# Row maxima to the stacked queries: a copy for all heads and one-hot key rows, in place of two DMAs per step

## What is computed

```python
x = x + _L0_xattn_ref(_layernorm(x), ctx_1024, ctx_1024)
x = x + _L0_ffn_ref(_layernorm(x), ...)       # 64 experts, top 8
x = x + _L1_xattn_ref(_layernorm(x), ctx_1024, Wq, Wk, Wv, Wo)   # causal
x = x + _L1_ffn_ref(_layernorm(x), ...)
# both attentions:
scores = jnp.einsum('bqhd,bkhd->bhqk', q, k) * scale
out = jnp.einsum('bhqk,bkhd->bhqd', jax.nn.softmax(scores, axis=-1), v)
```

## Time and profile before

| | |
|---|---|
| profiled execution | 1326.34 us |
| its span, first to last instruction | 1324.5 us |
| mean granted TensorE clock | 0.848 |
| median of three runs | 1323.26 us |
| TensorE busy, share | 971.9 us, 73% |
| VectorE busy, share | 614.0 us, 46% |
| ScalarE busy, share | 361.3 us, 27% |
| GpSimd busy, share | 487.8 us, 37% |
| first attention, first to last scores | 78.5 to 279 us |
| second attention, first to last scores | 926.9 to 1135 us |

### The profile page before, as it was taken

How to read it: one execution, slowest core, us unless ns; L and a number is a source line. 1 busy time by engine, 2 the same in 40 slices (tenths; PEclk the granted TensorE clock), 3 DMA queues, 4 the chain that set the end, 5 groups by cost and what they waited for, 6 DMA issues and landing times. The chain is left out here.

```text
span 1324.5 us, 22383 instructions
## 1 busy us (share of the span) xinstructions
PE 971.9 (73%) x5670; PEld 644.4 (49%) x5671; DVE 614.0 (46%) x1831; ACT 361.3 (27%) x884; POOL 487.8 (37%) x500
## 2 busy tenths in 40 slices
PE   4658687661003999999999999932667688589999
PEld 3525344430002666666666666622455466346665
DVE  4548776745001444444444444415777675232230
ACT  4526444430001222122222222210244345222221
POOL 4500332455563767676767767610000000000000
PEclk9959867865555999999999999975688789779999
DMA  5954564200004555665665666424556532200000
GB/s 179 294 140 135 78 89 67 45 21 11 0 0 122 182 179 189 188 195 165 189 196 182 205 206 198 153 102 167 156 153 195 156 92 70 78 0 16 17 15 17
DMA packets 78845, 160.32 MB, mean 121 GB/s; under 512 B 18448, under 2 KB 44048, under 8 KB 76480
## 3 DMA queue, kind: packets, MB, share of 16 engines
q1 hardware_dynamic: 59264, 112.16, 30.0%
q0 software_dynamic: 19520, 47.41, 11.5%
HBM read 118.09 MB, written 41.16 MB: 120 GB/s over the span
## 5 line engine op out<-in xcount | busy, mean ns | idle before, releaser
L1204 PE MATMUL ex_ps<-ex_w_gu,ex_rows_t 128*128 x640 | 263.2, 493 | 27.5 <-issue 17.0
L834 POOL DMA_INDIRECT expert_lists<-rt_number,rt_idx x128 | 124.4, 972 | 200.2 <-DMA expert_lists<-rt_number,rt_idx 116.0
L1173 POOL DMA_INDIRECT expert_outs<-ex_result,slot_places x160 | 158.7, 992 | 100.4 <-DVE ex_result L1316 98.3
L649 ACT ACTIVATE a_probs<-a_ps 128x512 f32<-128x512 f32 (+1 forms) x256 | 133.7, 541 | 167.6 <-PE a_ps L514 84.5
L494 PE MATMUL a_ps<-stacked_keys,a_qst 96*128 96x256 bf16 (+1 forms) x512 | 119.2, 307 | 77.9 <-DMA stacked_keys<-k_stack 57.6
L1168 POOL DMA_INDIRECT ex_rows<-moe_rows,slot_tokens x160 | 155.1, 970 | 56.9 <-issue 48.8
L1223 PE MATMUL ex_ps<-ex_w_down,ex_hidden_t 96*128 x640 | 166.8, 383 | 1.0 <-DVE ex_hidden_t L1308 1.0
L1658 POOL TENSOR_TENSOR x<-x,ff_b 128x256 f32 x16 | 11.5, 747 | 387.1 <-DVE ff_xn L1814 387.1
L1278 ACT ACTIVATE ex_act_g<-ex_ps 128x192 f32<-128x192 f32 x160 | 52.8, 330 | 353.7 <-PE ex_ps L1204 353.7
L511 PE MATMUL a_ps<-a_qst,stacked_keys 98*128 98x256 bf16 (+1 forms) x512 | 114.8, 298 | 27.8 <-DMA a_qst<-a_maxrows 18.7
L1204 PEld LDWEIGHTS ex_ps<-ex_w_gu,ex_rows_t 128*128 128x128 f32 x640 | 108.5, 192 | 43.3 <-issue 36.1
(11 more groups left out here) (210 smaller groups left out, 1341.6 us busy)
## 6 DMA issues: line engine op xcount, KB each, us to landing
ex_w_gu<-in_w_gu_dram SPq DMA_DIRECT2D x64, 384.0 KB, 3.2
cb_gathered<-expert_outs SPq DMA_DIRECT2D x16, 1024.0 KB, 7.7
ex_w_down<-in_w_down_dram SPq DMA_DIRECT2D x64, 192.0 KB, 3.7
k_stack<-split_parts SPq DMA_DIRECT2D x16, 384.0 KB, 2.6
a_qst<-q_stack SPq DMA_DIRECT2D x32, 192.0 KB, 4.5
stacked_keys<-k_stack SPq DMA_DIRECT2D x32, 192.0 KB, 4.6
a_qst<-q_stack SPq DMA_DIRECT2D x32, 128.0 KB, 4.4
stacked_keys<-k_stack SPq DMA_DIRECT2D x32, 128.0 KB, 4.4
```

The source lines that it names most:

```text
L649: nc.scalar.activation(probs[:, s, 0:cols], ps[:, 2 + s % 2, 0:cols], ACT.Exp, scale=scale).then_inc(exped, 1)
L834: nc.gpsimd.indirect_dma_start(k.lists, bass.IndirectOffsetOnAxis(ap=self.idx[:, t, s:s + 1], axis=0), self.number[:, t, s:s + 1], None).t ...
L1173: nc.gpsimd.indirect_dma_start(k.outs, bass.IndirectOffsetOnAxis(ap=k.places[:, begin + t:begin + t + 1], axis=0), result[:, t % R], None) ...
L1204: last = pe.matmul(ps[:, 2 + j % 2, 0:2 * FF], rows_t[:, j % 2, c * P:(c + 1) * P], w_gu[:, bass.ds(ring, 1), c, :].rearrange("p a n -> p ...
```

## The change

`MROWS` becomes 16: all 16 rows of the transposed maxima (2 parts x 8 heads) become rows 96 to 111 of `qst`. ScalarE copies them there from PSUM directly, the same 16 x 256 block for each head of the step, in two instructions of four heads each (16 x 1024 values). Since every head's queries then carry the maxima of all eight heads, the key side picks: rows 96 to 111 of `kst` are one-hot by head, 1 in the two rows of the own head. GpSimd makes them once, at the start of the first attention, with four `tensor_tensor` additions of broadcast columns of the bf16 identity (16 x 2048 each), ahead of its iotas; the memset of ones in `prepare` goes. The tile `maxrows`, the semaphores `max_in`, SyncE's wait and its two DMAs per step go. TensorE's transpose lands on partitions 96 to 111 and moves from s=4 to s=3, ahead of the side work of that slot; ScalarE's two copies stand at s=3 and s=4. `scores_kq` waits for the copies at s=0 and s=4, in the first attention also once per buffer for the one-hot rows; its product now runs over 112 rows.

```diff
--- before.py
+++ after.py
@@ -23,7 +23,7 @@
 STEPS = 2 * BATCH
 TERMS = 6
 ROWS = TERMS * DH
-MROWS = 2
+MROWS = 2 * HSTEP
 VW = 32
 EPS = 1e-5
 MASKED = -1e30
@@ -152,7 +152,6 @@
         c_in = [sem("ctx_in0"), sem("ctx_in1")]
         own = sem("own")
         eps_set = sem("eps_set")
-        ones_set = sem("ones_set")
         moments_ready = sem("moments")
         deviations = sem("deviations")
         xn_ready = sem("xn_ready")
@@ -298,8 +297,6 @@
                 nc.gpsimd.memset(eps[:], EPS).then_inc(eps_set, 1)
 
                 pool.wait_ge(eps_set, 1)
-                nc.gpsimd.memset(k.kst[ROWS:ROWS + MROWS], 1.0).then_inc(ones_set, 1)
-                pool.wait_ge(ones_set, 1)
 
                 def low(b, u, kind):
                     pool.wait_ge(middle, 3 * b + kind + 1)
@@ -371,7 +368,6 @@
         blockmax = sb("blockmax", [P, 2, HSTEP, 3], F32)
         negmax = sb("negmax", [P, 2, 2, HSTEP], F32)
         maxparts = sb("maxparts", [P, 2, 2, 2, HSTEP], BF16)
-        maxrows = sb("maxrows", [2 * HSTEP, 2, SEQ], BF16)
         turned_in = sb("turned_in", [P, 2, SEQ], F32)
         recip = sb("recip", [P, 2, HSTEP], F32)
         ps = ctx.enter_context(nc.psum_tensor(f"{name}_ps", [P, 8, 512], F32))
@@ -380,12 +376,12 @@
         QK_BANKS = (0, 1, 5)
         STACK_LOADS = 16 * 2 * len(RUNS)
         outs_dq = ps[:, 6, 0:SEQ]
-        max_t = ps[0:2 * HSTEP, 6, SEQ:SEQ + P].bitcast(BF16)
+        max_t = ps[ROWS:ROWS + MROWS, 6, SEQ:SEQ + P].bitcast(BF16)
         outs_qd = ps[:, 7, :].rearrange("p (j n) -> p j n", j=2)
 
         stack_in = [sem(f"stack_in{j}") for j in range(4)]
         v_in = [sem("v_in0"), sem("v_in1")]
-        max_in = [sem(f"max_in{j}") for j in range(4)]
+        keys_marked = sem("keys_marked")
         v_ready = sem("v_ready")
         own = sem("own")
         cut_step = sem("cut_step")
@@ -460,13 +456,6 @@
 
                         wait(sp, t_ready, HSTEP * (number(st) - LAG))
                         load(after(st, 1))
-                    before = after(st, -1)
-                    if scores(before):
-                        sp.wait_ge(max_copied, number(before) + 1)
-                        v = before[1]
-                        for part in range(MROWS):
-                            sp.dma_start(qst[ROWS + part:ROWS + part + 1, v],
-                                         maxrows[part * HSTEP:(part + 1) * HSTEP, v % 2, :]).then_inc(max_in[v], 16)
                     side.sync(sp, st)
 
                 side.sync_first(sp, lambda: load((0, 0)))
@@ -476,6 +465,12 @@
 
             @block.gpsimd
             def _(pool):
+                if not causal:
+                    for u in range(4):
+                        heads = [k.ident_b[ROWS:ROWS + MROWS, ROWS + part * HSTEP:ROWS + (part + 1) * HSTEP].unsqueeze(2).to_broadcast([MROWS, HSTEP, SEQ])
+                                 for part in range(2)]
+                        nc.gpsimd.tensor_tensor(kst[ROWS:ROWS + MROWS, u], heads[0], heads[1], ALU.add).then_inc(keys_marked, 1)
+                        pool.wait_ge(keys_marked, u + 1)
                 side.gpsimd(pool)
 
             @block.tensor
@@ -501,8 +496,10 @@
                 def scores_kq(st, s):
                     i, u = st
                     h = number(st)
-                    if s == 0:
-                        pe.wait_ge(max_in[u], 32 * i + 32)
+                    if s % 4 == 0:
+                        pe.wait_ge(max_copied, 2 * h + 1 + s // 4)
+                    if not causal and s == 0 and isinstance(i, int) and i == 0:
+                        pe.wait_ge(keys_marked, u + 1)
                     wait(pe, exped, HSTEP * h + s - 1)
                     bank = ps[:, 2 + s % 2, :]
                     for j in range(2):
@@ -524,7 +521,7 @@
                     b_par = u // 2
                     if g == 0:
 
-                        pe.wait_ge(max_copied, min(h + LAG, STEPS) if isinstance(h, int) else h + LAG)
+                        pe.wait_ge(max_copied, 2 * min(h + LAG, STEPS) if isinstance(h, int) else 2 * h + 2 * LAG)
                     if g == 0 and u % 2 == 0:
                         pe.wait_ge(v_ready, batch_of(st) + 1)
                     for j in range(2):
@@ -567,7 +564,7 @@
                             outputs(after(t, -1), 1)
                         if s == 3 and scores(after(t, -1)):
                             turn_outputs(after(t, -1), 1)
-                        if s == 4 and scores(after(st, -1)):
+                        if s == 3 and scores(after(st, -1)):
                             turn_maxima(after(st, -1))
                         if s == 7 and scores(t):
                             outputs(t, 0)
@@ -664,13 +661,11 @@
                     wait(act, out_turned, 2 * h + g - 1)
                     nc.scalar.copy(turned_in[:, g, :], outs_dq).then_inc(out_copied, 1)
 
-                def copy_maxima(st):
+                def copy_maxima(st, g):
                     h, u = number(st), st[1]
                     act.wait_ge(max_turned, h + 1)
-                    old = after(st, -2)
-                    if scores(old):
-                        act.wait_ge(max_in[old[1]], 32 * old[0] + 32)
-                    nc.scalar.copy(maxrows[:, u % 2, :], max_t).then_inc(max_copied, 1)
+                    nc.scalar.copy(qst[ROWS:ROWS + MROWS, u, 4 * g:4 * g + 4, :],
+                                   max_t.unsqueeze(1).to_broadcast([MROWS, 4, SEQ])).then_inc(max_copied, 1)
 
                 act.wait_ge(own, 2)
                 side.scalar_first(act)
@@ -682,8 +677,8 @@
                             exponential(t, s)
                         if s == 2 and scores(after(t, -1)):
                             copy_outputs(after(t, -1), 1)
-                        if s == 3 and scores(after(st, -1)):
-                            copy_maxima(after(st, -1))
+                        if s in (3, 4) and scores(after(st, -1)):
+                            copy_maxima(after(st, -1), s - 3)
                         if s == 5 and st[1] % 2 and scores(st):
                             copy_values(st)
                         if s == 7 and scores(t):
```

## The result

The changed kernel takes 1330.49 us in the median of 12 runs (1324.53 to 1339.84), the kernel before 1322.55 in 12 runs of the same comparison: ratio 1.0066, 95% interval 1.0034 to 1.0098. That is 7 to 9 us, less than the 1% that the prediction had called the limit, but clear of noise, and in the other direction than a removed wait suggests.

The account below looks back on a forecast made before the run. GpSimd's scatters were taken to cover the first attention from 134 us, leaving 4.0 us of waits on the path. Terms +2.4 - 0.5 - 0.3 = +1.6 us gave 1327.9 profiled, 1325 us as median; range 1311 to 1338.

Parts of the forecast that it names:

- What lies on the path: TensorE's waits for maximum rows before key-side scores: of 22.6 us, 18.6 covered by scatters, only 4.0 on the path.
- The copy's price: ScalarE's 16x1024 copies: about 1015 ns each, 0.09 us overlap with neighbours, +1.58 us a step; ScalarE-bound steps grow about 1.0.
- First attention, up to the first scatter: Steps 2 to 5 before GpSimd's scatters start: ScalarE's copies lengthen them, less a 0.4 us wait; +2.4 us.
- the 140 that I had set as a sign of being wrong: Start of GpSimd's scatters: first scatter expected near 136.5; before 134 or after 140 shows the forecast wrong.
- First attention, after it: Stretch paced by scatters: attention ending earlier gives some time back; -0.5 us, bounds -5.8 and +1.
- Second attention: -2.7 us in the two-step loop, +2.4 us in steps 11 to 16; net -0.3 us.
- Covered: One-hot additions on GpSimd, about 4.6 us each, hidden before the first key-side scores: 0, up to 0.8 us if contended.
- A: Key-side scores: waits for maxima come back whole, 22.6 us, giving 1301; chance 0.14.
- B: Copies between exponentials 3 and 5: ScalarE becomes the bound, +18.4 us, 1342, if a copy costs above about 1.5; chance 0.15.
- C: GpSimd's one-hot blocks are late, holding blank lists and the load behind; +6.6 us at 10 us each, 1331; chance 0.03.
- D: Each removed wait reappears as the wait for the same step's load; nothing moves, 1323; chance 0.10.
- many ScalarE waits at line 511: TensorE before the key-side scores: many waits for ScalarE there were to show the forecast wrong.

Follow-up runs that it names:

- first_only: Changed kernel's new way in the first attention only, the second keeping narrow copy and DMAs: 1329.20 us, ratio 1.0043 to the kernel before.
- the two groups above: Profiled kernels by first 32 scatters: four with the old way in the first attention, 84.8 to 91.9 us; six others of the same comparisons, 94.4 to 103.2.
- pairs: Changed kernel with its wide copies taken as 32-bit words (16x512 in place of 16x1024): 1319.70 us, ratio 0.9993 to the kernel before.
- second_only: Changed kernel's new way in the second attention only, the first keeping narrow copy and two DMAs: 1324.29 us, ratio 1.0019 to the kernel before.
- pairs_again: Changed kernel with its copies as 32-bit words, run once more: 1318.01 us, ratio 1.0012 to the kernel before.
- turn_only: Kernel before with only the transpose of the maxima moved to s=3, DMAs and narrow copies kept: 1313.02 us, ratio 0.9972.
- late_turn: Changed kernel with the transpose of the maxima back at s=4, copies where they are: 1371.44 us in four executions, ratio 1.0207 to the kernel before.
- marks_early: Changed kernel with the four one-hot additions in the preparation instead of at the start of the first attention: 1357.24 us, ratio 1.0109 to the kernel before.
- no_maxima: Changed kernel without key-side maxima: no copies or waits for them, products over 96 rows: 1337.66 us, ratio 0.9979 to the kernel before.
- double: Changed kernel with each wide copy done a second time into a spare tile: 1410.79 us, ratio 1.0540 to the kernel before.

## Why the prediction was right, and where not

The time lies in the range (1311 to 1338) and within 1% of before, as the likeliest case had it; but the sum was +1.6 us and it was +7 to +9. The range held by its width and not by its terms: the forecast's largest terms were too small or of the wrong sign, and the dear copies that its upper end stood for did not come.

- **What lies on the path**: right. Of 22.6 us of waits nearly nothing came back, and leaving copies and waits out gains 0.2%, at most 0.6%.
- **The copy's price**: 1004 ns against 1015, right; the overlap of 0.09 us with its neighbours was wrong where these are exponentials, and a step grew by 1.5 us at full clock, not 1.0.
- **First attention, up to the first scatter**, +2.4: too small by more than half. +3.1 in first_only, +6.3 and +6.6 in the two profiles of the changed kernel, whose first scatter (140.09) is past the 140 that I had set as a sign of being wrong. TensorE idles 5.3 us longer in first_only and 5.4 in the changed kernel, where I had 2.4; the rest is its clock, which differs by execution and which I left out.
- **First attention, after it**, -0.5 with bounds -5.8 and +1: this is the step that failed, in sign and outside its bounds. By the two groups above the first 32 scatters take 10 us longer in the mean (98.0 against 88.2), and the kernel's own two profiles lie above that. I reasoned that an earlier end of attention gives the scatters quiet time back. In the changed kernel attention does not end earlier (last exponential at 293 us, before at 289). Where it does, by 29 us in pairs against second_only and by 25 in pairs_again against turn_only, the rest of the chain is only 4.8 and 0.8 us shorter, and the first 32 scatters had lost 12.1 and 4.7. What slows these is open.
- **Second attention**, -0.3: -1.1 and +1.1 in two profiles, second_only's ratio 1.0019; right in its net. The parts behind it were too small on both sides: copies that would cost much (late_turn +19.8) are hidden by the move of the transpose, to which I gave 0.5 us a step.
- **Covered**: the one-hot additions, right (marks_early), though not as I had it: I looked at line 606 and 0.8 us, and it was the cast in front of it that stood for 2.25. SyncE's freed queue brought nothing visible.
- **Rivals**: A fell with no_maxima. B, ScalarE as the bound, is half true: it decides the first attention's early steps, and at twice the copies nearly every step (double). Its point, a copy above about 1.5 us, is consistent with that. C and D fell.
- My rule for TensorE's waits held as a reading: "many ScalarE waits at line 511" was to show the forecast wrong, and they came, 5.1 to 27.0 us, and with them the loss.

Two readings from the Trainium skill stand beside this. "SBUF — State Buffer", Who interferes with whom: a VectorE instruction with two SBUF inputs contends with a GpSimd instruction that reads SBUF. By that I expected the subtraction of line 606 to be held for 0.8 us at most; the trace shows the cast in front of it held for 2.25 us instead, and the fill shows no cost of it beyond 1 us. "DMA: Bandwidth & Descriptors", Queues, rings and completion order: a semaphore lands only after earlier writes of its DMA engine; no run here separates that from plain sharing.

## What to carry to other kernels

Removing a wait that is not on the path can still slow what is: here the small indirect DMAs on the path took 10 us longer beside an attention without its waits. Before removing one, ask which path-bound transfer runs beside it, and after the change measure that one by itself, in equal time, before naming a cause. When a copy is added to an engine that works in order, do not count on overlap at its seams (at those with exponentials there was none here), and put its producer as early in the other engine's order as its data allows; that position was worth 20 us beside copies of 32 us in the second attention. And a bf16 block can be copied at half the width as 32-bit words; for which bit patterns that loses nothing was not looked into here.

## What was not expected of the hardware

- ScalarE's copy from PSUM costs by element count, not by bytes: 16x1024 bf16 1004 ns, the same bytes as 16x512 fp32 577 ns. Exponentials follow each other in some 0.5 us for 0.60 of duration, and two wide copies in 0.91 for 1.00, but a wide copy and an exponential follow without overlap (0.62 and 1.03 us).
- VectorE's SBUF copy with a broadcast source, 16x1792 bf16, took 1082 ns, 0.6 ns per element.
- GpSimd's addition of two broadcast bf16 columns to 16x2048 took 3.6 us, 1.76 ns per element, where the fp32 subtraction of the earlier trace rows takes 2.26.
- A 128x16 cast of VectorE beside GpSimd's additions took 1.63 to 2.49 us instead of 0.17 in six profiles, until the addition ended.
- The same step with the same instructions took 9.1 or 11.1 us as the granted clock was 1.00 or 0.81; the mean granted clock of the whole fill was 0.78 before and after the change.
